# The reciprocal of the softmax row sums: VectorE's RECIPROCAL, or GpSimd's power with exponent -1

## The reference, cut to what matters

```python
scores = einsum('bhid,bhjd->bhij', q, k) * SCALE + einsum('bhid,ijd->bhij', q, rel_k)
threshold = top_k(scores, 32)[0][..., -1:]
scores = where(scores < threshold, -inf, scores)
attn = softmax(scores, axis=-1)          # exp(s - max) / sum
for i in range(3):                       # three powers of attn, applied to v
    v_curr = attn @ v_curr  (+ attn with rel_v, for i == 0)
    res = res + sigmoid(alphas[i]) * v_curr
out = res @ Wout.T + bout                # then x + out, layer norm, feed-forward, residual
```

## Time and profile before

| | us |
|---|---|
| median of 3 runs | 737.08 |
| lowest, highest | 735.47, 737.32 |
| the profiled execution | 735.55 |
| its span in the trace | 733.8 |

### The profile page before, as it was taken

One profiled execution on the slowest core, in us unless ns is written; L12 is line 12 of the kernel. 1 busy time (PEld: TensorE's weight loads), 2 busy tenths in 40 slices (PEclk: granted clock), 3 DMA queues, 4 the chain that ended last, 5 costly groups with the idle time before them and its releaser, 6 DMA issues.

```text
span 733.8 us, 20797 instructions
## 1 busy us (share of the span) xinstructions
PE 658.8 (90%) x5736; PEld 513.3 (70%) x5736; DVE 678.7 (92%) x2823; ACT 618.9 (84%) x1756; POOL 542.4 (74%) x935
## 2 busy tenths in 40 slices
PE   4477889999999999999999999999999999987784
PEld 3355777777777777777777777777777777765673
DVE  5998989999999999999999999999999999998325
ACT  3668788989999899989999899989999899988523
POOL 1588878877878778777787777878777787777621
PEclk9779999999999999999999999999999999999898
DMA  6735444445455444545544554444444444443102
GB/s 202 185 106 153 127 129 143 148 130 146 135 157 149 131 141 138 158 129 150 145 133 135 152 151 128 151 147 140 149 130 150 147 142 148 147 132 84 48 8 57
DMA packets 148338, 98.72 MB, mean 135 GB/s; under 512 B 10624, under 2 KB 147968, under 8 KB 148096
## 3 DMA queue, kind: packets, MB, share of 16 engines
q1 hardware_dynamic: 147920, 97.32, 45.2%
q10 hardware_dynamic: 304, 0.08, 0.0%
HBM read 45.59 MB, written 51.77 MB: 133 GB/s over the span
## 4 chain that ended last, share of the span: by engine, by line
DVE 73%; issue 11%; POOL 7%; PE 4%; ACT 2%; DMA 2%; SPq 0%; ACTq 0%; POOLq 0%; DVEq 0%
DVE top L679 37%; DVE work L685 32%; POOL s_sb L322 3%; POOL s_sb L297 1%; DMA band_scratch<-zeros 1%; DVE rinv L666 1%; ACT a_sb L447 1%; PE ps_y L895 1%; POOL wk L365 1%; POOL x_sb L370 1%; POOL a_sb L327 1%; ACT pen L437 1%; DVE stats L702 1%; PE ps_p L880 1%; PE ps_s L958 0%
## 5 line engine op out<-in xcount | busy, mean ns | idle before, releaser
L679 DVE MAX8 top<-work 128x8 f32<-128x256 f32 x768 | 284.7, 413 | 0.0
L322 POOL TENSOR_TENSOR s_sb<-s_sb,pen 128x512 f32<-128x512 f32 x128 | 163.2, 1275 | 58.8 <-ACT pen L437 58.8
L685 DVE MATCH_REPLACE8 work<-top,work 128x256 f32<-128x256 f32 x512 | 205.9, 410 | 0.0
L327 POOL TENSOR_SCALAR a_sb<-a_sb,rinv 128x256 f32<-128x256 f32 x256 | 119.7, 478 | 58.3 <-DVE rinv L666 57.7
L447 ACT ACTIVATE a_sb<-s_sb,nmax 128x256 f32<-128x256 f32 x256 | 128.1, 501 | 35.6 <-POOL s_sb L322 27.6
L437 ACT ACTIVATE pen<-s_sb,limit 128x256 f32<-128x256 f32 x256 | 117.4, 512 | 35.3 <-POOL limit L309 35.3
L880 PE MATMUL ps_p<-aT,rows 128*64 128x256 f32 x1024 | 124.9, 385 | 8.3 <-ACT rows L511 3.5
L297 POOL TENSOR_TENSOR s_sb<-s_sb,skew 128x384 f32<-128x384 f32 x128 | 128.3, 1002 | 2.8 <-DMA skew<-band_scratch 2.8
L685 DVE MATCH_REPLACE8 work<-top,s_sb 128x256 f32<-128x256 f32 x256 | 102.9, 410 | 0.0
L880 PEld LDWEIGHTS ps_p<-aT,rows 128*64 128x64 f32 x1024 | 70.2, 136 | 45.4 <-issue 15.7
L679 DVE MAX8 top<-s_sb 128x8 f32<-128x256 f32 x256 | 94.4, 411 | 3.8 <-POOL s_sb L297 3.8
(11 more groups left out here) (134 smaller groups left out, 1286.2 us busy)
## 6 DMA issues: line engine op xcount, KB each, us to landing
skew<-band_scratch SPq DMA_DIRECT2D x128, 192.0 KB, 2.7
diag_scratch<-a_sb SPq DMA_DIRECT2D x128, 192.0 KB, 2.3
band_scratch<-band SPq DMA_DIRECT2D x128, 191.0 KB, 3.4
diag<-diag_scratch SPq DMA_DIRECT2D x128, 128.0 KB, 2.2
wqkv<-in_wqkv SPq DMA_DIRECT2D x1, 1152.0 KB, 8.2
x_sb<-in_x SPq DMA_DIRECT2D x4, 256.0 KB, 5.1
wout<-in_wout SPq DMA_DIRECT2D x1, 512.0 KB, 5.5
out<-xn SPq DMA_DIRECT2D x1, 512.0 KB, 3.3
```

The lines of the kernel that those rows point to most:

```text
L322: nc.gpsimd.tensor_tensor(s_sb[g % 4][:], s_sb[g % 4][:], pen[g % 2][:], ALU.subtract).then_inc(pen_added, 1)
L327: nc.gpsimd.tensor_scalar(a_sb[g % 3][:, t, :], a_sb[g % 3][:, t, :], rinv[g % 2][:, t:t + 1], 1.0, ALU.mult, ALU.mult).then_inc(normed, 1)
L679: nc.vector.max(m[:, t, 8 * n:8 * n + 8], src).then_inc(top_step, 1)
L685: nc.vector.match_replace(work[t][:, n % 2, :], m[:, t, 8 * n:8 * n + 8], src, LOW).then_inc(top_step, 1)
```

## The change

`divide` and its 128 RECIPROCALs leave DVE's queue. `normalise` on POOL first waits for the exponentials, forms `rinv = rsum ** -1` as a TENSOR_TENSOR with a constant tile `minus` of -1.0, counts the same semaphore `rinv_done`, and waits for it itself. One MEMSET for `minus` is added at the start.

```diff
+            nc.gpsimd.memset(minus[:], -1.0).then_inc(made, 1)
+            pool.wait_ge(made, MADE)
             def normalise(g):
+                pool.wait_ge(exp_done, T * (g + 1))
+                reach(pool, normed, T * (g - 1))
+                nc.gpsimd.tensor_tensor(rinv[g % 2][:], rsum[g % 2][:], minus[:], ALU.pow).then_inc(rinv_done, 1)
                 pool.wait_ge(rinv_done, g + 1)
-            def divide(g):
-                dve.wait_ge(exp_done, T * (g + 1))
-                reach(dve, normed, T * (g - 1))
-                nc.vector.reciprocal(rinv[g % 2][:], rsum[g % 2][:]).then_inc(rinv_done, 1)
...
-                    if n == 2 and g > 0:
-                        divide(g - 1)
-            divide(HEADS - 1)
```

## The result

The changed kernel takes 781.52 us (median; 780.21 to 782.45), the kernel before, measured beside it, 737.07: a ratio of 1.0607, 95% interval 1.0584 to 1.063, +44.5 us. The forecast was +10 us, 746, with a range up to 800. The direction held, the size did not.

What follows compares the result with a forecast made beforehand. DVE was taken to bound the even stretch by 0.03 us a slot over a POOL and ACT loop, which the power lengthens. 26.2 - 17.5 + 1.2 = +9.9 us on 735.55, called 746; range 729 to 800.

Steps and rivals of the forecast that it cites:

- The bound before: Even stretch, 120 to 672 us: DVE needs 10.06 us a slot (a pair of heads), POOL and ACT together 10.03.
- the loop: POOL and ACT waiting for each other from one even head's normalise to the next: 10.03 us without `add_bout`, 11.28 with.
- The slot as 9.88 + x: Time of a head pair through POOL and ACT after the change: 10.03 - 0.31 + 0.16 + x, x being the power's time.
- x - 0.41 more for the odd head: Odd head's power on POOL: free up to 0.41 us; beyond that it adds x - 0.41 a slot.
- the odd head's slack: Behind the odd head's normalise, POOL's limit ends before ACT needs it for the ramp: 0.38 us free.
- The size of x: Time of one 128x2 power on POOL: 0.19 us plus 0.12 for each of two columns, 0.43; bounds 0.19 and 1.275.
- the forecast's own sum: Whole kernel: 61 x - 17.5, and 61 (x - 0.41) more where x is above 0.41; +9.9 us at 0.43.
- The projection's pauses: Seven times in the even stretch the projection holds up DVE's MAX8 by 1.07 us; 1.1 us in all charged as unhidden.
- DVE's gain alone: Two reciprocals a slot leave DVE, 0.08 us each: 9.90 instead of 10.06 us, 8.6 us over 54 slots.
- The footing: Sums start from the profiled execution, 735.55 us, against a median of 737.08; 1.5 us to be added at the end.
- a pause at a first power: Rival at POOL's first power: some 6 us for a first call, forecast then 752; chance 0.03.
- The cheap case: Rival: a power on POOL takes 0.19 to 0.25 us, kernel faster by 5.9 to 2.3 us, 728.5 to 733; chance 0.25.

Runs made afterwards that it cites:

- the product: Changed kernel with POOL's power made a product at the same place, division left out: 732.47 us against 736.83 for the kernel before, ratio 0.9947.
- the row of the sizes: Changed kernel with ten more instructions at POOL's start, powers of 1 to 64 columns and products of 2 to 64, into spare tiles: one execution, 801.03 us.
- an order that gives POOL room: Changed kernel with POOL's limit(g+1) between power(g) and normalise(g), clip directly behind the odd penalty: 728.31 us; same order on the kernel before: 727.90.
- the three orders tried: POOL reordered, with power/reciprocal: limit ahead of power and normalise 763.08/761.53 us; limit between them, clip behind even limit 746.06/747.95; clip behind odd penalty 728.31/727.90.

## Why the prediction was wrong

- *The bound before* (DVE by 0.03 us a slot over the loop): that the two are all but equal held, and that a pause on DVE then fell on the path (11.16 against 10.07). The margin of 0.03 itself is not shown: the product at x = 0.20 gave a slot of 10.11, the formula 10.08, and the power for even heads alone 10.64, the formula 10.58, so the formula is short by as much as the margin or twice that.
- *The slot as 9.88 + x, and x - 0.41 more for the odd head:* held within 0.06. With the measured 0.70 it gives 9.88 + 0.70 + 0.29 = 10.87; measured 10.91. POOL's wait for itself was 0.10 instead of 0.08, and stands twice in the slot once the odd head's slack is used.
- *The size of x:* this is the step that failed. The prediction said "0.12 us for each of the two columns beside the 0.19, so x = 0.43"; it measured 0.14 for each beside 0.42. The price of a column was near. The error is the fixed part, which I took from the additions and the product-like TENSOR_SCALARs; a power pays 0.23 us more before its first column. Put into the forecast's own sum, 61 x 0.70 - 17.5 + 61 x 0.29 = +42.9 us, against the measured 44.5.
- *Why 0.27 us in x made 33 us, 61 x 2 x 0.27:* up to 0.41 only one head in two pays; beyond, both. I took a value 0.02 past that bend as the centre, so an error upwards counted twice.
- *The projection's pauses:* I charged 1.1 us for the part that might not be hidden; it was nothing.
- *DVE's gain alone, 8.6 us:* too large by a third; a reciprocal costs DVE 0.06 us, so it is 6.5. It never entered the sum, as DVE was not the bound.
- *The footing:* the 1.5 us between the profiled execution and the median went into the 746 alone, not into the rivals' times or the ends of the ranges (729, 738, 800), which should all lie 1.5 us higher. It decides nothing here.
- *The rivals:* no pause at a first power was seen in the row of the sizes. The cheap case was real as a mechanism: the product showed it, -4.4 us for a forecast of -5.9. On saturated DVE and work moved to GpSimd (the Trainium skill, Perfetto Trace Analysis, Optimizing Scalar/DVE Operations): the rows bear the rule out only for an operation of 0.20 us, with 4.4 us gained. With a power in the old order the move loses 6%, and with an order that gives POOL room it neither gains nor loses (728.31 and 727.90).

## What to carry to other kernels

An instruction on an engine that the page of the profile shows at 74% can set the whole time, if two engines wait for each other through it: measure the loop, not the share, and do so in a stretch where it is already the bound, less what is extra there. When the price of an operation that the trace has never shown is guessed from its neighbours, its fixed part is as unknown as its price per column. And where the cost curve bends close to the chosen value, as it did here at 0.41, an error to the steeper side counts more, so the centre should lean to that side. The order of a queue was worth more here (8 us, with either reciprocal) than the place of the reciprocal; but each instruction that changes places has its own readers, and two of the three orders tried lost before the third won.

## What the runs showed of the hardware

- A power on GpSimd takes 0.57 us for one column of 128 partitions, 0.70 for two, 10.55 for 64: 0.42 fixed and 0.14 to 0.16 a column. The product of the same shapes takes 0.19 and 0.32.
- The distance from a GpSimd instruction's end to the next one that waits for its semaphore was 0.10 us behind the power, 0.07 behind a MEMSET.
- A 128x2 reciprocal between VectorE's MAX8s costs it 0.06 us of its slot (10.07 against 9.95 for two), well under half of the 0.157 us of its row.
